# Perceiver block on one core: first chunks loaded one by one into four banks, and another order of TensorE's products in three steps of the self attention

## The chip, the core and the metric

The kernel runs on one core of a Trainium2 chip. The engines named below are TensorE (PE in the profile, PEld its weight loads), VectorE (DVE), ScalarE (ACT), GpSimd (POOL) and SyncE (SP, which here only issues DMAs). The metric is the device time of one execution in microseconds, lower is better.

## The reference

x is 8 sequences of 128 rows of 512, the context 8 x 2048 rows of 512. Three residual layers follow each other, each behind a layer norm:

```python
x = x + xattn(layernorm(x), ctx)   # q = x@Wq, k = ctx@Wk, v = ctx@Wv, 8 heads of 64, softmax, @Wo + bo
x = x + attn(layernorm(x))         # 8 heads in 2 groups, k and v through 32 latent columns, causal softmax, @wo
x = x + ffn(layernorm(x))          # gelu(x@W1)@W2 for all, and 2 of 8 experts for each row by its gate
```

All is float32. Where a product must be exact to about float32 and cheap, an operand is split in a rounded part (`_h`) and a rest (`_l`), and three products of the rounded type replace one.

## The kernel before

Every engine has its own written program, and semaphores join them; nothing reorders the work. The program has three parts: cross attention (to about 1045 us of the trace), self attention with the shared feed forward of the first six sequences (to about 1241 us), and the experts.

**Start of the cross attention.** The context comes in groups of 512 rows, a group in two parts of 512 KB (`load_ctx`, L217), each with two of the four 128-row chunks of the contraction; `stage[:, 0]` and `stage[:, 1]` hold the raw parts in turn. For the first group SP loads half of Wv, part 0, the other half, part 1 (L241 on). ScalarE rounds each as it lands (`first_part`, L605), VectorE makes the rest (L742, L745), counted by `wv_split` and `first_split`. TensorE's `project_v` (L401) makes a tile of 128 rows of values: 4 chunks x 3 products (`three`, L367), in one of two banks `ps_p` (`pair_ps` in the rows); `await_bank` lets it go on when the copy out of that bank, two tiles back, is done. `arrive_first` makes the first tile wait for each half. ScalarE copies tile 0, rounds parts 2 and 3 of the second group (`round_ctx`, L675), and then copies tiles 1 to 3 (`copy_v`, L626). GpSimd splits parts 2 and 3 (L300). Behind the first tile of the second group TensorE transposes x (`turn_x`, L483).

**Self attention.** Eight PSUM banks are handed around by a table: `fills(name, bank)` states in which order names fill a bank, `await_empty`, `await_filled` and `await_copied` wait by it. Before the loop over the eight sequences TensorE folds the weights (`fold_query_weights`, `turn_folded`, and `fold_out_weight` L1228, which makes `wol` from Wo), makes value latents of four sequences (`latents`, products with `wvd`), queries of four sequences (`queries`, products of `wql` and `xnT`, one half per bank and 8 products each in the rows' count), and scores of sequence 0. Half 1 stands for sequences 4 to 7. In step s of the loop: `turn_probs(s)` (transposes of `stage`), `scores(s+1)` (mask and L1272), `mix(s)` (L1291), `self_out(s)` (products with `wol`), `turn_norm` of the new row block (`x3T`, transposes of `xn`), `gate(s)` (products with `wg`), and `rank(s-1)` (L1308, L1309), which gives rows their places with the experts. Mixed in are the shared feed forward of earlier sequences: `up_high` and `up_low` of sequence s-1 (L1326, L1329, L1337), `turn_gelu`, `down_high` and `down_low` of sequence s-2 (L1354, L1361, L1364). Between self_out and x3T stand, on VectorE, the sum and its statistics, on GpSimd the root, and on VectorE the norm (L1570 to L1582); between `gate(s-1)` and `rank(s-1)` stand ScalarE's exponentials and VectorE's `choose` (L1711 on), which VectorE reaches only behind the norm of step s.

## Time and profile before

| | |
|---|---|
| median of 3 runs | 1548.08 us (1547.4 to 1550.31) |
| the profiled execution | 1547.3 us |
| its span | 1545.4 us |
| TensorE busy | 1503.8 us, 97% |
| VectorE, ScalarE, GpSimd busy | 723.2, 710.4 and 706.5 us |
| mean granted clock of TensorE | 0.994 |

The span runs from the first to the last instruction; the execution has 1.9 us around it. A matmul counts as busy from its issue to its modelled end, so neighbours overlap, and a row of the timeline that merges n of them lasts longer than the distance between their starts. Idle time in square brackets is that just before the row, with the instruction that ended it. An fp32 matmul of the program is two in the rows.

### The profile page before, as it was taken

The page shows a single profiled execution, that of the slowest core. Times are in us where ns is not written, and L with a number is a line of the kernel's source. Part 1 is how long each engine was busy: PE and PEld are TensorE (multiplying, and loading weights), DVE is VectorE, ACT ScalarE, POOL GpSimd, SP SyncE. Part 2 cuts the span into 40 slices and gives each one's busy share as a digit, 9 for nine tenths or more (in the row PEclk, how much of TensorE's full clock was granted, in tenths as well). Part 3 has the DMA queues.
Part 4 walks back from the last instruction along what each step waited for, and adds up shares of the span by engine and source line. Part 5 has one row for each costly group of instructions (what it writes and reads, how often), then busy time and mean ns, then how long its engine had stood idle before and what let it go on. Part 6 is the DMA issues. An engine that isn't in the chain of part 4 may idle for free. (4 is left out here: it accounts for less than half of the span.)

```text
span 1545.4 us, 25507 instructions
## 1 busy us (share of the span) xinstructions
PE 1503.8 (97%) x9986; PEld 1212.6 (78%) x9987; DVE 723.2 (47%) x1100; ACT 710.4 (46%) x1197; POOL 706.5 (46%) x559
## 2 busy tenths in 40 slices
PE   7999999999999999999999999989889999999997
PEld 5678888888888888888888888865567777888886
DVE  4124533632731822732543453393365565567552
ACT  3244544543644544454454454344466554454531
POOL 3112941851752572481392293076421116688651
PEclk9999999999999999999999999999899999999999
DMA  6111041022114103103104103115100076567522
GB/s 218 61 56 36 28 123 43 28 87 72 35 35 125 35 28 116 49 23 109 62 1 131 47 16 112 40 56 192 42 28 28 28 275 182 144 195 195 154 38 37
DMA packets 57446, 127.85 MB, mean 83 GB/s; under 512 B 7104, under 2 KB 11264, under 8 KB 57344
## 3 DMA queue, kind: packets, MB, share of 16 engines
q1 hardware_dynamic: 48672, 109.81, 22.0%
q0 software_dynamic: 4304, 8.44, 2.9%
q10 hardware_dynamic: 4368, 8.18, 1.8%
q8 instruction: 71, 1.16, 0.3%
q14 instruction: 31, 0.25, 0.1%
HBM read 94.22 MB, written 33.24 MB: 82 GB/s over the span
## 5 line engine op out<-in xcount | busy, mean ns | idle before, releaser
L300 POOL TENSOR_TENSOR ctx_l<-stage,ctx_h 128x1024 fp32r<-128x1024 f32 x62 | 147.5, 2401 | 481.9 <-ACT ctx_h L675 481.9
L367 PE MATMUL pair_ps<-wv,ctx_h 128*128 128x512 f32 x1024 | 323.4, 397 | 10.8 <-DVE ctx_l L745 9.3
L367 PE MATMUL pair_ps<-ctx_h,wk 128*128 128x512 f32 x1024 | 331.2, 394 | 0.0
L783 DVE TENSOR_TENSOR s_top<-ps_s,s_top 128x512 f32<-128x512 f32 x192 | 121.2, 684 | 338.8 <-ACT s L644 338.8
L367 PEld LDWEIGHTS pair_ps<-wv,ctx_h 128*128 128x128 f32 x1024 | 187.9, 188 | 54.0 <-issue 9.9
L367 PEld LDWEIGHTS pair_ps<-ctx_h,wk 128*128 128x128 f32 x1024 | 192.2, 188 | 42.7 <-issue 1.2
L626 ACT ACTIVATE vt<-pair_ps 128x512 f32<-128x512 f32 x128 | 76.5, 598 | 274.4 <-PE pair_ps L367 213.3
L367 PE MATMUL pair_ps<-wv,ctx_l 128*128 128x512 f32 x512 | 200.3, 391 | 0.0
L367 PE MATMUL pair_ps<-ctx_l,wk 128*128 128x512 f32 x512 | 199.5, 390 | 0.0
L644 ACT ACTIVATE s<-ps_s 128x512 f32<-128x512 f32 x256 | 133.0, 602 | 61.0 <-PE ps_s L420 36.6
L620 ACT ACTIVATE kT<-pair_ps 128x512 f32<-128x512 f32 x128 | 76.6, 598 | 176.7 <-PE pair_ps L367 176.7
L420 PEld LDWEIGHTS ps_s<-qT,kT 64*128 64x128 f32 x2048 | 119.3, 188 | 19.2 <-issue 16.5
L420 PE MATMUL ps_s<-qT,kT 64*128 64x128 f32 x2048 | 131.5, 278 | 0.0
L651 ACT ACTIVATE s<-s 128x1024 f32<-128x1024 f32 x128 | 125.8, 1049 | 4.6 <-DVE s L813 4.6
L785 DVE COPY s_top<-ps_s 128x512 f32<-128x512 f32 x64 | 40.4, 685 | 175.0 <-ACT s L644 175.0
L449 PEld LDWEIGHTS ps_o<-s,vt 128*64 128x64 f32 x2048 | 111.6, 137 | 5.0 <-issue 2.8
L449 PE MATMUL ps_o<-s,vt 128*64 128x128 f32 x2048 | 114.2, 273 | 1.2 <-ACT s L651 1.2
L367 PEld LDWEIGHTS pair_ps<-wv,ctx_l 128*128 128x128 f32 x512 | 96.5, 188 | 20.8
L367 PEld LDWEIGHTS pair_ps<-ctx_l,wk 128*128 128x128 f32 x512 | 96.2, 188 | 19.7 <-issue 1.2
L813 DVE TENSOR_TENSOR s<-s,ps_s 128x2048 f32<-128x2048 f32 x48 | 106.1, 2276 | 0.0
L2027 ACT ACTIVATE wxo<-pair_ps 128x512 f32<-128x512 f32 x46 | 27.6, 599 | 142.9 <-PE pair_ps L1967 142.3
L1876 POOL TENSOR_TENSOR lu<-raw_u,hu 128x1024 fp32r<-128x1024 f32 x28 | 69.2, 2815 | 28.5 <-ACT hd L2021 28.5
(295 smaller groups left out, 2323.2 us busy)
## 6 DMA issues: line engine op xcount, KB each, us to landing
stage<-in_ctx_dram SPq DMA_DIRECT2D x64, 512.0 KB, 4.1
rows_scratch<-bo SPq DMA_DIRECT2D x66, 258.5 KB, 4.7
raw_u<-in_up_dram SPq DMA_DIRECT2D x32, 512.0 KB, 3.9
stage<-in_down_dram SPq DMA_DIRECT2D x16, 512.0 KB
raw_e<-in_down_dram SPq DMA_DIRECT2D x16, 512.0 KB, 4.2
bo<-rows_scratch ACTq DMA_DIRECT2D x22, 258.5 KB, 3.2
s<-in_x_dram SPq DMA_DIRECT2D x2, 1024.0 KB, 11.5
q_scratch<-s SPq DMA_DIRECT2D x2, 1024.0 KB, 4.6
```

The lines of the kernel that those rows point to most:

```text
L300: nc.gpsimd.tensor_tensor(lo, raw, hi, ALU.subtract).then_inc(done, 1)
L367: mm = nc.tensor.matmul(out, w(c), m(c), start=(c + k == 0), stop=(c == DC - 1 and k == 2))
L420: mm = nc.tensor.matmul(ps_e[:, 2 * (n % 2) + e, i], kT[rows, p, i * P:(i + 1) * P], qT[rows, p, :], start=True, stop=True)
L449: mm = nc.tensor.matmul(ps_o[e * XD:(e + 1) * XD, p, :], vt[:, (b * MT + t) % RING, h * XD:(h + 1) * XD], s[:, h, t, :], start=(t == 0), s ...
L620: nc.scalar.activation(kT[:, p, :], ps_p[:, NTH[b, "K", g, p] % 2], ACT.Copy).then_inc(k_copied, 1)
L626: nc.scalar.activation(vt[:, nth_v(b, g, t) % RING, :], ps_p[:, NTH[b, "V", g, t] % 2], ACT.Copy) \
L644: nc.scalar.activation(s[:, 2 * p + e, 4 * g:4 * g + 4, :], ps_e[:, 2 * (n % 2) + e], ACT.Copy) \
L651: nc.scalar.activation(part, part, ACT.Exp, scale=X_SCALE).then_inc(exp_done, 1)
L783: ins = nc.vector.tensor_tensor(top[:, p, e], bank, top[:, p, e], ALU.max)
L785: ins = nc.vector.tensor_copy(top[:, p, e], bank)
L813: nc.vector.tensor_tensor(s[:, h], s[:, h], largest_score, ALU.subtract).then_inc(shifted, 1)
L1876: nc.gpsimd.tensor_tensor(weight_chunk(lu[s % 2], ld[s % 2], i), raw_part(i), weight_chunk(hu[s % 2], hd[s % 2], i), ALU.subtract).then_in ...
```

## The change

The first two chunks of Wv and of the context are loaded in four DMAs of 256 KB, each with a semaphore, and rounded and split singly; the other two chunks stay a pair. `first_values` takes chunk after chunk over all four tiles, which stand in four banks at once (`first_room`: two of `ps_p`, two of `ps_s`). So ScalarE copies all four at the end, behind the rounding of parts 2 and 3. Part 2 is loaded when the second chunk is split, part 3 when the last pair is.

In the self attention the folding of Wo moves behind the first scores, and its copies from ScalarE to VectorE. The first latents stand in two halves between other steps; the second latents move ahead of the loop, and half of the second queries into step 0 in their place. In step 1 `up_high(0, 0)` goes ahead of self_out and the rest of that sequence's up products ahead of `turn_norm`; from step 2 on the order is that of before. ScalarE rounds x3T of sequence 0 in step 0 (step 1 before), VectorE takes its rest ahead of the maxima of step 1. In the steps with a `down_high` that now stands ahead of `rank` where both are in front of self_out, which is so in the last step alone. The bank table follows.

```diff
@@ -238,12 +243,14 @@
 
-            for i in range(2):
-                load_weight(wv_raw, wv_ap, i, wv_in)
-                load_ctx(0, i)
+            for c, w_in, c_in in ((0, wv_start, ctx_start), (1, wv_in[0], raw_in[0])):
+                sp.dma_start(wv_raw[:, c, :], wv_ap[c * P:(c + 1) * P, :]).then_inc(w_in, 16)
+                sp.dma_start(stage[:, 0, c, :], ctx_ap[0, 0, :, c, :]).then_inc(c_in, 16)
+            load_weight(wv_raw, wv_ap, 1, wv_in)
+            load_ctx(0, 1)
             sp.dma_start(x_all[:, 0:HB], x_ap[0:HB].rearrange("b t d -> t b d")).then_inc(x_in[0], 16)
             for k in range(2, 4):
-                sp.wait_ge(first_split, k - 1)
+                sp.wait_ge(first_split, k)
@@ -369,17 +376,28 @@
 
-                if n >= 2:
+                if n in (4, 5):
+                    pe.wait_ge(v_copied, n - 3)
+                elif n >= 2:
                     b, kind, g, i = MADE[n - 2]
                     if kind == "K":
                         pe.wait_ge(k_copied, nth_k(b, g, i) + 1)
                     else:
                         pe.wait_ge(v_copied, nth_v(b, g, i) + 1)
 
-            def arrive_first(c):
-                if c % 2 == 0:
-                    pe.wait_ge(wv_split, c // 2 + 1)
-                    pe.wait_ge(first_split, c // 2 + 1)
+            def first_values():
+
+                for c in range(DC):
+                    if c < 3:
+                        pe.wait_ge(wv_split, c + 1)
+                        pe.wait_ge(first_split, c + 1)
+                    for t in range(4):
+                        rows = slice(t * P, (t + 1) * P)
+                        for k, (i, j) in enumerate(((ctx_h, 0), (ctx_l, 0), (ctx_h, 1))):
+                            mm = nc.tensor.matmul(first_room(t), i[:, 0, c, rows], wv[:, j, c, :], start=(c + k == 0),
+                                                  stop=(c == DC - 1 and k == 2))
+                        if c == DC - 1:
+                            mm.then_inc(proj_done, 1)
...
@@ -623,7 +640,8 @@
                     act.wait_ge(pv_done, PAIRS * (b if g or t == 3 else b - 1))
-                nc.scalar.activation(vt[:, nth_v(b, g, t) % RING, :], ps_p[:, NTH[b, "V", g, t] % 2], ACT.Copy) \
+                made = ps_p[:, NTH[b, "V", g, t] % 2] if b + g else first_room(t)
+                nc.scalar.activation(vt[:, nth_v(b, g, t) % RING, :], made, ACT.Copy) \
@@ -674,13 +692,13 @@
 
-            for i in range(2):
-                part = slice(2 * i, 2 * i + 2)
-                first_part(wv[:, 0, part, :], wv_raw[:, part, :], wv_in[i])
-                first_part(ctx_h[:, 0, part, :], stage[:, i], raw_in[i])
-            copy_v(0, 0, 0)
+            for c, w_in, c_in in ((0, wv_start, ctx_start), (1, wv_in[0], raw_in[0])):
+                first_part(wv[:, 0, c, :], wv_raw[:, c, :], w_in)
+                first_part(ctx_h[:, 0, c, :], stage[:, 0, c, :], c_in)
+            first_part(wv[:, 0, 2:4, :], wv_raw[:, 2:4, :], wv_in[1])
+            first_part(ctx_h[:, 0, 2:4, :], stage[:, 1], raw_in[1])
             round_ctx(0, (2, 3))
-            for t in range(1, 4):
+            for t in range(4):
@@ -736,13 +754,13 @@
 
-            for i in range(2):
-                part = slice(2 * i, 2 * i + 2)
+            for i, part in enumerate((slice(0, 1), slice(1, 2), slice(2, 4))):
+                raw = stage[:, 1] if i == 2 else stage[:, 0, part, :]
                 dve.wait_ge(first_hi, 2 * i + 1)
                 nc.vector.tensor_tensor(wv[:, 1, part, :], wv_raw[:, part, :], wv[:, 0, part, :], ALU.subtract) \
                     .then_inc(wv_split, 1)
                 dve.wait_ge(first_hi, 2 * i + 2)
-                nc.vector.tensor_tensor(ctx_l[:, 0, part, :], stage[:, i], ctx_h[:, 0, part, :], ALU.subtract) \
+                nc.vector.tensor_tensor(ctx_l[:, 0, part, :], raw, ctx_h[:, 0, part, :], ALU.subtract) \
...
@@ -1388,21 +1410,23 @@
             fold_query_weights(1)
-            pe.wait_ge(wo_in, 16)
             turn_folded(0)
-            fold_out_weight(0)
+            pe.wait_ge(wkv_in, 32)
+            latents(0, range(0, HB // 2))
             turn_folded(1)
-            fold_out_weight(1)
-            pe.wait_ge(wkv_in, 32)
-            latents(0)
+            latents(0, range(HB // 2, HB))
             for ro in range(2):
                 await_copied(pe, f"wql{ro}")
-            queries(0)
+            queries(0, range(SKV))
             pe.wait_ge(rounded, 2)
             scores(0)
+            pe.wait_ge(wo_in, 16)
+            for g in range(SKV):
+                fold_out_weight(g)
             for s in range(HB, B):
                 await_copied(pe, f"xT{s}")
-            queries(1)
+            queries(1, range(0, 1))
+            latents(1)
@@ -1415,26 +1439,32 @@
                 mix(s)
+                if 0 <= late < EARLY:
+                    down_high(late)
                 if s == B - 1:
                     rank(s - 1)
-                if 0 <= late < EARLY:
-                    down_high(late)
                 if s == 0:
                     keys(1)
+                if s == LAG:
+                    up_high(0, 0)
                 self_out(s)
                 if s == 0:
-                    latents(1)
+                    queries(1, range(1, SKV))
                 if 0 <= late < EARLY:
                     down_low(late)
-                if 0 <= soon < EARLY:
+                if 0 < soon < EARLY:
                     up_high(soon, 0)
+                if s == LAG:
+                    up_high(0, 1)
+                    up_low(0, 0)
+                    up_low(0, 1)
                 turn_norm(f"x3T{s}", s, B + s + 1)
-                if 0 <= soon < EARLY:
+                if 0 < soon < EARLY:
                     up_high(soon, 1)
                 if 0 < s < B - 1:
                     rank(s - 1)
                 gate(s)
-                if 0 <= soon < EARLY:
+                if 0 < soon < EARLY:
@@ -1506,14 +1536,12 @@
                 take(f"wql{n}", wql[:, :, n, :])
-                take(f"wol{n}", wol[:, n, :])
             take("vl0", vl[:, 0:HB])
             for ro in range(2):
                 take(f"ql0{ro}", qlT[:, ro, 0:HB * T])
             exps(0)
             normalise(0)
-            for ro in range(2):
-                take(f"ql1{ro}", qlT[:, ro, HB * T:B * T])
+            take("ql10", qlT[:, 0, HB * T:B * T])
@@ -1529,14 +1557,18 @@
                     take("vl1", vl[:, HB:B])
-                if 0 <= soon < EARLY:
-                    if soon:
-                        await_filled(act, f"up{soon - 1}{NH - 1}")
+                if 0 < soon < EARLY:
+                    await_filled(act, f"up{soon - 1}{NH - 1}")
                     await_copied(act, f"x3T{soon}")
                     nc.scalar.activation(rowT_h[:, :, :], x3T[:, soon % 2], ACT.Copy).then_inc(rowTh_done, 1)
                 if s + 1 < B:
                     normalise(s + 1)
+                if s == 0:
+                    take("ql11", qlT[:, 1, HB * T:B * T])
                 take(f"x3T{s}", x3T[:, s % 2])
+                if s == 0:
+                    await_copied(act, "x3T0")
+                    nc.scalar.activation(rowT_h[:, :, :], x3T[:, 0], ACT.Copy).then_inc(rowTh_done, 1)
@@ -1614,10 +1646,16 @@
             invert(0)
+            for g in range(SKV):
+                take(f"wol{g}", wol[:, g, :])
             dve.wait_ge(on_set, 3)
             for s in range(B):
                 late, soon = s - LAG - 1, s - LAG
                 take(f"pT{s}1", pT[:, 1])
+                if s == LAG:
+                    dve.wait_ge(rowTh_done, 1)
+                    nc.vector.tensor_tensor(rowT_l[:, :, :], x3T[:, 0], rowT_h[:, :, :], ALU.subtract) \
+                        .then_inc(rowTl_done, 1)
...
```

The order of the instructions is shown in three places. ScalarE, start of the cross attention, before:

```order
L605 ACTIVATE wv<-vt 128x1024 [waits wv_in0]
L605 ACTIVATE ctx_h<-stage 128x1024 [waits raw_in0]
L605 ACTIVATE wv<-vt 128x1024 [waits wv_in1]
L605 ACTIVATE ctx_h<-stage 128x1024 [waits raw_in1]
L626 ACTIVATE vt<-pair_ps 128x512 [waits proj_done]
L675 ACTIVATE ctx_h<-stage 128x1024 [waits raw_in0]
L675 ACTIVATE ctx_h<-stage 128x1024 [waits raw_in1]
L626 ACTIVATE vt<-pair_ps 128x512 [waits proj_done] x3
```

and now (rows of `vt` are the copies of value tiles, `wk` the rounding of Wk):

```order
L622 ACTIVATE wv<-vt 128x512 [waits wv_start]
L622 ACTIVATE ctx_h<-stage 128x512 [waits ctx_start]
L622 ACTIVATE wv<-vt 128x512 [waits wv_in0]
L622 ACTIVATE ctx_h<-stage 128x512 [waits raw_in0]
L622 ACTIVATE wv<-vt 128x1024 [waits wv_in1]
L622 ACTIVATE ctx_h<-stage 128x1024 [waits raw_in1]
L693 ACTIVATE ctx_h<-stage 128x1024 [waits raw_in0]
L693 ACTIVATE ctx_h<-stage 128x1024 [waits raw_in1]
L644 ACTIVATE vt<-pair_ps 128x512 [waits proj_done] x2
L644 ACTIVATE vt<-ps_s 128x512 [waits proj_done] x2
```

The first copy stood ahead of both later roundings of `ctx_h`; now all four stand behind them.

TensorE from the latents ahead of the loop to the end of step 0's self_out and what follows it, before (`xnT,wql` are queries, `wvd,xnT` latents, `wo,wupT` folding of Wo, `xnT,wkd` keys, `wol,o_mid` self_out):

```order
L1170 MATMUL pair_ps<-wvd,xnT 128x64 x16
L1170 MATMUL bank<-xnT,wql 128x512 x8
L1267 MATMUL bank<-mask_r,ident2r 128x512 x2
L1272 MATMUL bank<-wq,qlT 128x256 x4
L1170 MATMUL bank<-xnT,wql 128x512 x8
L1175 MATMUL bank<-ident,stage 128x128 x8
L1267 MATMUL bank<-mask_r,ident2r 128x512 x2
L1272 MATMUL bank<-wq,qlT 128x256 x4
L1291 MATMUL pair_ps<-o_mid,vl 32x128 x8
L1170 MATMUL bank<-xnT,wkd 128x512 x4
L1170 MATMUL pair_ps<-wol,o_mid 128x512 x2
L1170 MATMUL pair_ps<-wvd,xnT 128x64 x16
```

and now, from the second pair of products of the first scores on:

```order
L1294 MATMUL bank<-wq,qlT 128x256 x4
L1248 MATMUL pair_ps<-wo,wupT 32x512 x4
L1248 MATMUL bank<-wo,wupT 32x512 x4
L1190 MATMUL bank<-xnT,wql 128x512 x4
L1190 MATMUL pair_ps<-wvd,xnT 128x64 x16
L1195 MATMUL bank<-ident,stage 128x128 x8
L1289 MATMUL bank<-mask_r,ident2r 128x512 x2
L1294 MATMUL bank<-wq,qlT 128x256 x4
L1313 MATMUL pair_ps<-o_mid,vl 32x128 x8
L1190 MATMUL bank<-xnT,wkd 128x512 x4
L1190 MATMUL pair_ps<-wol,o_mid 128x512 x2
L1190 MATMUL bank<-xnT,wql 128x512 x4
```

The folding, half of the queries and the second latents now stand between the first scores and the transposes of the probabilities (`ident,stage`); behind self_out stand four products of queries where sixteen small ones of latents stood.

TensorE from the mix of step 1 to the transposes of step 2, before (`hu`, `lu` are the up products, `ident,xn` the transposes for x3T, `both,on` and `heap,on` rank, `wg,wqlT` gate):

```order
L1291 MATMUL pair_ps<-o_mid,vl 32x128 x8
L1170 MATMUL pair_ps<-wol,o_mid 128x512 x2
L1326 MATMUL bank<-hu,rowT_h 128x512 x4
L1329 MATMUL bank<-hu,rowT_l 128x512 x4
L1175 MATMUL bank<-ident,xn 128x128 x4
L1326 MATMUL bank<-hu,rowT_h 128x512 x4
L1329 MATMUL bank<-hu,rowT_l 128x512 x4
L1308 MATMUL pair_ps<-both,on 128x8
L1309 MATMUL pair_ps<-heap,on 128x8
L1170 MATMUL pair_ps<-wg,wqlT 128x8 x4
L1337 MATMUL bank<-lu,rowT_h 128x512 x8
```

and now:

```order
L1313 MATMUL pair_ps<-o_mid,vl 32x128 x8
L1348 MATMUL bank<-hu,rowT_h 128x512 x4
L1351 MATMUL bank<-hu,rowT_l 128x512 x4
L1190 MATMUL pair_ps<-wol,o_mid 128x512 x2
L1348 MATMUL bank<-hu,rowT_h 128x512 x4
L1351 MATMUL bank<-hu,rowT_l 128x512 x4
L1359 MATMUL bank<-lu,rowT_h 128x512 x8
L1195 MATMUL bank<-ident,xn 128x128 x4
L1330 MATMUL pair_ps<-both,on 128x8
L1331 MATMUL pair_ps<-heap,on 128x8
L1190 MATMUL pair_ps<-wg,wqlT 128x8 x4
```

All up products now stand ahead of the transposes of x3T; between these and rank, and between gate and the next step, nothing is left.

## Rows read from the trace of the kernel before

**Rows 1.** the timeline of the start: start us, us, engine, line, operation, count [idle before]
```profile
4.93 1.06 ACT L605 ACTIVATE wv<-vt 128x1024 fp32r<-128x1024 f32 x1 [2.90 <-DMA vt<-in_xv_dram]
...
6.89 1.06 ACT L605 ACTIVATE ctx_h<-stage 128x1024 fp32r<-128x1024 f32 x1 [0.90 <-DMA stage<-in_ctx_dram]
7.98 1.23 DVE L745 TENSOR_TENSOR ctx_l<-stage,ctx_h 128x1024 fp32r<-128x1024 f32 x1 [0.73 <-ACT ctx_h L605]
...
9.35 1.19 PE L367 MATMUL pair_ps<-wv,ctx_h 128*128 128x512 f32 x2 [9.35 <-DVE ctx_l L745]
...
10.63 1.23 DVE L745 TENSOR_TENSOR ctx_l<-stage,ctx_h 128x1024 fp32r<-128x1024 f32 x1
...
14.01 0.60 ACT L626 ACTIVATE vt<-pair_ps 128x512 f32<-128x512 f32 x1 [3.41 <-PE pair_ps L367]
```

**Rows 2.** the windows: line 367 alone from 14 to 19 us: length, PE busy, PEld busy, PEclk
```profile
14.00:19.00 5.00, 5.00 (x23) 4.13 (x23) 1.00 0.83 243
```

**Rows 3.** the timeline again, where the second context group begins
```profile
19.22 1.06 ACT L675 ACTIVATE ctx_h<-stage 128x1024 fp32r<-128x1024 f32 x1 [3.66 <-DMA stage<-in_ctx_dram]
20.19 1.07 ACT L626 ACTIVATE vt<-pair_ps 128x512 f32<-128x512 f32 x2
20.36 2.42 POOL L300 TENSOR_TENSOR ctx_l<-stage,ctx_h 128x1024 fp32r<-128x1024 f32 x1 [1.32 <-ACT ctx_h L675]
...
20.82 0.73 PE L367 MATMUL pair_ps<-wv,ctx_h 128*128 128x512 f32 x2 [1.40 <-ACT vt L626]
...
26.42 0.60 PE L483 MATMUL ps_m<-ident,s 128*128 128x128 f32 x4
```

**Rows 4.** TensorE's timeline, self attention, step 0 and ahead of it
```profile
1071.80 1.07 PE L1228 MATMUL bank<-wo,wupT 128*32 128x512 f32 x8
...
1087.27 7.13 PE L1170 MATMUL bank<-xnT,wql 128*128 128x512 f32 x16
1094.96 0.63 PE L1175 MATMUL bank<-ident,stage 128*128 128x128 f32 x4 [0.56 <-ACT stage L1479]
1096.13 0.63 PE L1175 MATMUL bank<-ident,stage 128*128 128x128 f32 x4 [0.54 <-ACT stage L1479]
...
1098.80 3.70 PE L1170 MATMUL bank<-xnT,wkd 128*128 128x512 f32 x8
...
1104.05 3.68 PE L1170 MATMUL pair_ps<-wvd,xnT 128*128 128x64 f32 x32
```

**Rows 5.** TensorE's timeline from the end of step 0 to step 2
```profile
1109.01 1.09 PE L1175 MATMUL bank<-ident,xn 128*128 128x128 f32 x4 [1.27 <-DVE xn L1582]
1111.11 1.85 PE L1170 MATMUL pair_ps<-wg,wqlT 128*128 128x8 f32 x8 [1.02 <-ACT wqlT L1452]
...
1119.82 1.95 PE L1170 MATMUL pair_ps<-wol,o_mid 128*128 128x512 f32 x4 [1.19 <-DVE o_mid L1564]
...
1127.41 0.63 PE L1175 MATMUL bank<-ident,xn 128*128 128x128 f32 x4 [3.16 <-DVE xn L1582]
...
1130.34 0.36 PE L1308 MATMUL pair_ps<-both,on 128*128 128x8 f32 x2 [0.47 <-DVE both L1716]
...
1133.61 1.03 PE L1175 MATMUL bank<-ident,stage 128*128 128x128 f32 x8
```

**Rows 6.** the timeline of VectorE and of ScalarE in step 0
```profile
1106.75 2.11 DVE L1582 TENSOR_SCALAR xn<-x_soon,mv,rstd 128x512 f32<-128x512 f32 x1 [0.67 <-POOL rstd L1157]
...
1108.05 2.44 ACT L1479 ACTIVATE stage<-stage,inv 128x128 f32<-128x128 f32 x8
```

**Rows 7.** the windows of all engines, for the granted clock (PEclk)
```profile
1108.00:1120.00 12.00, 8.79 (x47) 6.51 (x48) 3.98 (x10) 5.17 (x21) 2.98 (x2) 0.57 0.01 1
1245.00:1250.00 5.00, 5.00 (x20) 4.03 (x19) 1.27 (x8) 0.44 (x1) 0.31 (x1) 0.66 0.94 313
```

**Rows 8.** TensorE's timeline, last step of the self attention
```profile
1231.26 0.36 PE L1308 MATMUL bank<-both,on 128*128 128x8 f32 x2 [1.16 <-issue]
```

**Rows 9.** DMA issues: count, KB each, median us to landing
```profile
qT<-q_scratch SPq DMA_DIRECT2D x7, 256.0 KB, 2.9
```

33 lines of the change are left out of this document (20 added, 13 removed).

## The prediction

> **What bounds the kernel now.** I read the page first: TensorE is busy in nearly every slice, so the time is TensorE's work plus the places where it waits or runs at the lower clock. Then the waits of TensorE (who was waited for), which sent me to three stretches, and there the timeline, engine by engine; last the windows for the granted clock and the list of DMA issues. Four things are to be seen.
>
> At the start TensorE does nothing until 9.35: half of Wv and half of the first context group (512 KB each) are landed, rounded on ScalarE and split on VectorE in turn, 1.06 and 1.23 us apiece [rows 1]. Twelve products of the first tile then take from 9.35 to 14.01. Later 23 of them touch 5.0 us, so 22 starts, 0.227 apart [rows 2], so twelve would take 2.7: the cold start costs 1.9.
>
> Then, at 20.82, TensorE has waited 1.40 for a bank: ScalarE's copies of the value tiles stand behind the rounding of context part 3, whose transfer lands at 19.22 [rows 3].
>
> In steps 0 and 1 of the self attention TensorE waits seven times in rows of the timeline: 0.56 and 0.54 for the first probabilities, 1.27 for xn of step 0, 1.02 for the copy of its transpose (ScalarE is in the normalisation of step 1 until 1110.4), then 1.19, 3.16 and 0.47 in step 1 [rows 4, 5, 6]. From 1108 to 1120 the granted clock has a mean of 0.57, where it has 0.50 (1.2 GHz) or 1.00 (2.4 GHz) at a time: (1 - 0.57) / 0.5 x 12 = some 10.2 us at the lower level [rows 7].
>
> In the last step TensorE waits 1.16 for the choice of step 6 before `rank` [rows 8].
>
> **The change, part by part.** The profiled execution took 1547.3 us, span 1545.4 and 1.9 around it; the median before, 1548.1, is 0.8 above. All sums are made against 1547.3.
>
> *First chunks.* The first two DMAs become 256 KB each. A 256 KB load elsewhere lands in a median of 2.9 us [rows 9]; issued at 0.75 and 1.24 the second would be there at 4.1 at best, and at 4.9 at worst (ScalarE starts the first whole 512 KB part at 4.93). I take 4.9, because these loads start the queue. Half of 1.06 and half of 1.23, with 0.1 between, give 6.3 to 6.4 for the first product instead of 9.35: 3.0 earlier. The cold stretch is paid as before. Chunk 0 feeds 12 products (four banks), cold for 8 of them: to about 10.7; chunk 1 is split near 8.2 (1 MB are there at 6.89, then half of 1.06 and of 1.23), and chunks 2 and 3 at 11.86 as before [rows 1] (their transfers are not moved), when TensorE is still in chunk 1. So 48 products end at 6.4 + 1.9 + 48 x 0.227 = 19.2. No wait between.
>
> What is late next is part 3 again: it is requested after the last first split (third count now, second before), which is the same moment, so it lands at 19.2 as before. ScalarE now has both roundings ahead of all four copies, so: rounding to 20.3, first copy to 20.8, and TensorE can begin group 1 at 20.9; two of its four chunks take it to 22.3, and GpSimd's split of part 3 is done at 22.8 [rows 3]. The tile then ends at 22.8 + 1.4 = 24.2. Before, the x transposes behind the same tile began at 26.42. Gain 2.2. Behind the copies on ScalarE stands only the rounding of Wk, which waits for its own transfer. Everything after this in the cross attention is TensorE's own length, so the 2.2 should reach the end. Bounds: if part 3 still lands so late that TensorE needs it 1 us more, 1.2; if, with part 2 requested 1 us earlier, it lands before 17, then the end of the 48 products decides and the gain is 4.5.
>
> *Step 0.* The folding of Wo (two groups of 1.0 to 1.1) goes from before the queries to behind scores 0; so scores 0 end at 1085.3 instead of 1087.3 and the probabilities come 2.0 earlier. TensorE now has, behind them, folding 2.1, half of the second queries 3.3 (7.13 for both, tail included) and latents 3.6 [rows 4]: to 1094.2. The probabilities were there at 1094.9 and 1096.1, now 1092.9 and 1094.1: both waits vanish. From the first transposes to the end of self_out took 1094.96 to 1104.05, that is 8.55 without the 0.54: self_out ends at 1102.7 (1.35 earlier). Only 3.3 of queries stand behind it now, to 1106.0. xn came 4.96 after self_out's end (1104.05 to 1109.01), of which 2.11 is one VectorE operation [rows 6]; I leave it so: 1107.7, a wait of 1.6 in place of 1.27. ScalarE's normalisation began when the copy of the latents let it (1108.05); latents are early now, so it ends near 1106.3, the new copy of queries near 1106.9, and the x3T copy follows its transposes: `gate` starts at 1108.8, not 1111.11, and ends at 1109.7. The copies of the folded Wo move to VectorE (some 0.6 each, half of the 1.23 of its 128x1024 form [rows 1]), behind the inverses of step 0, 3 us ahead of `mix`: nothing.
>
> *Step 1.* At full clock transposes, scores and mix take 3.3 (1094.96 to 1098.80 without the 0.54), to 1113.0; the first half of up_high, eight products of 0.227, covers the 1.19 for u and its own wait; self_out, 1.7, ends at 1116.5. Ahead of the next transposes stand 16 such products, 3.6, against 4.96 for xn: a wait of 1.4 at 1120.1 where 3.16 stood. But nothing now stands between the transposes and `rank`: the choice on VectorE came 2.93 after them (1127.41 to 1130.34), so TensorE goes idle for 2.5 there, to 1124.4; rank and gate are 1130.34 to 1133.61 less the 1.8 of up_low, 1.5: to 1125.9. Before, the next transposes began at 1133.61 [rows 5]. At full clock that is 7.7 gained. Some 3.6 of it is the low clock of before (of its 10.2 us TensorE was busy for about 7, half of that lost), 4.1 are waits and drained pipelines.
>
> *The clock.* The clock fell before where TensorE had short waits and narrow products, and again between 1245 and 1250, there for (1 - 0.66) / 0.5 x 5 = 3.4 us of dense work [rows 7]. The new kernel still has such a stretch at 1106 to 1109.7 (idle 1.6 and 0.8, eight-column products) and has a new one at 1120.1 to 1125.9. So I charge two low stretches of 3.4, each with TensorE busy through it: 2 x 1.7 = 3.4. Bounds: none (0) and four of them (6.8). Term for both steps: 7.7 - 3.4 = 4.3, from 0.9 to 7.7.
>
> The Trainium skill (TensorE: Matmul & The Clock Gate, Part 1) ties the fall of the clock to an idle engine and its release to activity. Taken as idleness alone, the 3.16 us wait should have been the place of the fall; here the clock stayed at 1.00 there and fell after a 1.27 us wait, so the trace disagrees with that reading. By idleness alone the new kernel, with 2.5 as its longest wait there, would lose nothing to the clock: that is the second rival.
>
> *Last step.* down_high (1.9) goes ahead of `rank`, so the 1.16 is covered; VectorE's placing of rows follows rank and still ends before self_out does. Gain 1.1; bounds 0 and 1.2.
>
> Sum: 2.2 + 4.3 + 1.1 = 7.6. 1547.3 - 7.6 = 1539.7, and with the 0.8 to the median **1540.5 us**.
>
> **Rivals.**
> A. Absorbed start: the transfer of part 3, or its split, ends the start as before or later, and the first term is at most 1.0; the rest holds. For it: the transfer is what ScalarE waits for at 19.22. Against: the tile behind had 2.7 us of work that is now ahead of it. 1541.7 to 1542.7. Chance 0.15.
> B. No low clock in steps 0 and 1 (and part 3 perhaps earlier): 1548.1 - (2.2 + 7.7 + 1.1) = 1537.1, down to 1534.8. Chance 0.2.
> C. More low clock, four stretches of 3.4: 1543.9. For it: the new weak stretch is 5.8 us long, and before, one fall lasted three times as long as the other. Chance 0.15.
> D. Slower: the new idle 2.5 before `rank`, with rank and gate behind it, keeps TensorE at 1.2 GHz well into steps 2 to 4, whose work has no slack. It must eat 2.2 + 7.7 + 1.1 = 11.0, at half a us per us: above 22 us of low clock (10.2 before) the kernel is slower; at 30 us it is 1552.1. Against it: the one fall followed by dense products was over in 3.4. Chance 0.03.
> E. The clocks fall on other phases in the last step and behind it, which moves any case by 1.7 either way.
>
> **Numbers.** Forecast 0.47, A 0.15, B 0.2, C 0.15, D 0.03. The forecast's own range is 1538.8 to 1542.2; to hold 8 in 10 it reaches to most of A, B and C: 1536 to 1544.5. A measurement tells 0.2%, 3.1 us, from no change: faster than 1545.0 is all but D and a tail of C with E: faster 0.90, same 0.07, slower 0.03.
>
> **What would show it.** The first product at 6.4; no wait until about 19.2 and then one near 1.7 for a ScalarE copy; x transposes at 24.2. No wait for the first probabilities; waits of about 1.6, 0.8, 1.4 and 2.5 in steps 0 and 1; no wait before the last rank; the steps 2 to 6 as long as before. Wrong would be: a first product after 8, the transposes of x after 26, or low-clock stretches of more than 10 us in total between 1090 and 1140.

## The result, and the profile after

| | before | after |
|---|---|---|
| median | 1548.51 us (4 runs, 1547.4 to 1550.31) | 1539.74 us (4 runs, 1538.26 to 1541.63) |
| the profiled execution | 1547.3 us | 1541.63 us |
| its span | 1545.4 us | 1539.8 us |

The ratio is 0.9944, with a 95% interval of 0.9932 to 0.9955: the change takes 8.8 us off. The forecast was 1540.5. The profiled execution of before was the fastest of its kernel and that of after the slowest, so the two profiles lie only 5.7 us apart. What sets the profile of after apart is more time at the lower clock in steps 0 and 1, below; its other three executions have no profile.

**The start.** The timeline of the changed kernel (start us, length us, engine, line, operation, count, and in brackets the idle time before and who ended it) against [rows 1] and [rows 3]:

```profile
3.36 0.63 ACT L622 ACTIVATE wv<-vt 128x512 fp32r<-128x512 f32 x1 [1.33 <-DMA vt<-in_xv_dram]
...
5.14 0.63 ACT L622 ACTIVATE ctx_h<-stage 128x512 fp32r<-128x512 f32 x1 [1.15 <-DMA stage<-in_ctx_dram]
5.80 0.69 DVE L763 TENSOR_TENSOR ctx_l<-stage,ctx_h 128x512 fp32r<-128x512 f32 x1 [1.09 <-ACT ctx_h L622]
...
6.64 0.77 PE L397 MATMUL pair_ps<-wv,ctx_h 128*128 128x512 f32 x1 [6.64 <-DVE ctx_l L763]
...
8.15 0.63 ACT L622 ACTIVATE ctx_h<-stage 128x512 fp32r<-128x512 f32 x1 [0.98 <-DMA stage<-in_ctx_dram]
```

```profile
17.43 1.06 ACT L693 ACTIVATE ctx_h<-stage 128x1024 fp32r<-128x1024 f32 x1 [1.70 <-DMA stage<-in_ctx_dram]
18.40 1.06 ACT L644 ACTIVATE vt<-pair_ps 128x512 f32<-128x512 f32 x2
...
19.35 2.36 POOL L307 TENSOR_TENSOR ctx_l<-stage,ctx_h 128x1024 fp32r<-128x1024 f32 x1
```

```profile
18.95 0.40 PE L397 MATMUL ps_s<-wv,ctx_h 128*128 128x512 f32 x1
19.19 0.63 PE L374 MATMUL pair_ps<-wv,ctx_h 128*128 128x512 f32 x2
...
21.76 0.72 PE L374 MATMUL pair_ps<-wv,ctx_h 128*128 128x512 f32 x2 [1.03 <-POOL ctx_l L307]
...
23.25 0.60 PE L501 MATMUL ps_m<-ident,s 128*128 128x128 f32 x4
```

The first product starts at 6.64 (6.4 was said), and the 48 products run without a wait to 19.19 (19.2). There is no wait for a ScalarE copy behind them, because part 3 landed at 17.43 and not at 19.22. What ends the start now is GpSimd's split of part 3, at 21.7. The x transposes begin at 23.25, 3.2 us earlier than in [rows 3], where 24.2 was said. The eight kernels measured here whose start is that of after begin them at 23.25 to 24.01, 23.5 on average, and the three with the old start at 26.10 to 26.42, 26.3 on average: 2.7 us is the better figure for this term.

**Steps 0 and 1.** TensorE's timeline against [rows 4] and [rows 5]:

```profile
1083.69 3.70 PE L1190 MATMUL bank<-xnT,wql 128*128 128x512 f32 x8
1087.23 3.68 PE L1190 MATMUL pair_ps<-wvd,xnT 128*128 128x64 f32 x32
1090.75 1.04 PE L1195 MATMUL bank<-ident,stage 128*128 128x128 f32 x8
...
1104.03 0.63 PE L1195 MATMUL bank<-ident,xn 128*128 128x128 f32 x4 [1.35 <-DVE xn L1614]
1105.43 1.66 PE L1190 MATMUL pair_ps<-wg,wqlT 128*128 128x8 f32 x8 [0.78 <-ACT wqlT L1482]
...
1121.24 0.63 PE L1195 MATMUL bank<-ident,xn 128*128 128x128 f32 x4 [1.17 <-DVE xn L1614]
```

```profile
1101.71 1.89 POOL L1167 TENSOR_TENSOR hd<-wq,one 128x1024 fp32r<-128x1024 f32 x1
1101.78 2.11 DVE L1614 TENSOR_SCALAR xn<-x_soon,mv,rstd 128x512 f32<-128x512 f32 x1 [0.66 <-POOL rstd L1177]
...
1118.99 2.11 DVE L1614 TENSOR_SCALAR xn<-x_soon,mv,rstd 128x512 f32<-128x512 f32 x1 [0.67 <-POOL rstd L1177]
...
1121.48 1.89 DVE L1751 CAST xn<-index 128x2 f32<-128x2 uint32 x1
```

The probabilities' waits are gone (the transposes at 1090.75 have no bracket). The four waits that the prediction named can be read from who waited for whom between 1097 and 1130 us (us in total, times, the longest):

```profile
PE bank L1195 <- DVE xn L1614: 2.5, 2, 1.4
PE pair_ps L1330 <- DVE both L1754: 2.3, 1, 2.3
PE pair_ps L1190 <- ACT wqlT L1482: 0.8, 1, 0.8
```

(The first row holds two waits.) That is 1.35 for x3T0, 0.8 for gate, 1.17 for x3T1 (the timeline's bracket) and 2.3 for the rank, where 1.6, 0.8, 1.4 and 2.5 were said. The rows of VectorE and GpSimd above show what stands in two of these chains: xn at 2.11, as in [rows 6], beside an operation of GpSimd that starts just before it, and a cast of two columns at 1.89.

**The clock.** The windows, 1100 to 1135 us: length, then busy time of PE, PEld, DVE, ACT and POOL, the mean granted clock, DMA share and GB/s:

```profile
1100.00:1135.00 35.00, 29.42 (x150) 20.97 (x149) 19.60 (x51) 19.45 (x64) 12.07 (x9) 0.80 0.04 16
```

(1 - 0.80) / 0.5 x 35 = 14 us at 1.2 GHz. The same window of the kernel before has 0.85, 10.5 us. So in this execution there was more low clock than before, not the two stretches of 3.4 that the forecast charged. In windows of 1 us it is 6.8 us from 1105.6 on, behind the waits of step 0, and 6.8 from 1122.7 on, from within the wait for the rank. The prediction named more than 10 us of low clock between 1090 and 1140 as a sign that it was wrong; in this execution the sign was there.

**The last step.** TensorE waits 0.47 for gT_h ahead of down_high, which was not foreseen, and the wait of 1.16 before rank [rows 8] is gone:

```profile
1223.91 0.65 PE L1313 MATMUL pair_ps<-o_mid,vl 128*32 128x128 f32 x16
1225.04 2.09 PE L1376 MATMUL pair_ps<-hd,gT_h 128*128 128x512 f32 x8 [0.47 <-ACT gT_h L1553]
1226.96 0.28 PE L1330 MATMUL bank<-both,on 128*128 128x8 f32 x2
...
1232.76 0.60 PE L1195 MATMUL bank<-ident,xn 128*128 128x128 f32 x4
```

### The profile page after: what moved, and what is told of

Same layout as the page of the kernel before. It is cut to its first block and busy times, and to the rows that moved or that the text cites. A ratio compares the mean times of both kernels' runs of the same rounds, so it can differ in the third digit from the quotient of the medians.

```text
span 1539.8 us, 25515 instructions
## 1 busy us (share of the span) xinstructions
PE 1504.3 (98%) x9986; PEld 1214.8 (79%) x9987; DVE 722.1 (47%) x1104; ACT 709.9 (46%) x1197; POOL 705.5 (46%) x559
## 3 DMA queue, kind: packets, MB, share of 16 engines
q8 instruction: 71, 1.16, 0.3%
## 5 line engine op out<-in xcount | busy, mean ns | idle before, releaser
L374 PE MATMUL pair_ps<-wv,ctx_h 128*128 128x512 f32 x992 | 312.1, 396 | 1.0 <-POOL ctx_l L307 1.0
L374 PEld LDWEIGHTS pair_ps<-wv,ctx_h 128*128 128x128 f32 x992 | 181.3, 188 | 43.0 <-POOL ctx_l L307 1.5
L374 PE MATMUL pair_ps<-wv,ctx_l 128*128 128x512 f32 x496 | 193.6, 390 | 0.0
L637 ACT ACTIVATE kT<-pair_ps 128x512 f32<-128x512 f32 x128 | 76.6, 598 | 177.1 <-PE pair_ps L374 177.1
L438 PEld LDWEIGHTS ps_s<-qT,kT 64*128 64x128 f32 x2048 | 119.3, 188 | 19.2 <-issue 16.5
L374 PEld LDWEIGHTS pair_ps<-ctx_l,wk 128*128 128x128 f32 x512 | 96.2, 188 | 19.7 <-issue 1.2
L374 PEld LDWEIGHTS pair_ps<-wv,ctx_l 128*128 128x128 f32 x496 | 93.1, 188 | 20.0
```

The costliest lines, as they stand in the source:

```text
L374: mm = nc.tensor.matmul(out, w(c), m(c), start=(c + k == 0), stop=(c == DC - 1 and k == 2))
L438: mm = nc.tensor.matmul(ps_e[:, 2 * (n % 2) + e, i], kT[rows, p, i * P:(i + 1) * P], qT[rows, p, :], start=True, stop=True)
L637: nc.scalar.activation(kT[:, p, :], ps_p[:, NTH[b, "K", g, p] % 2], ACT.Copy).then_inc(k_copied, 1)
```

## The experiments

Twelve kernels were run; ratios are to the kernel before, from runs on the same chip. To compare the profiles I use one length: from the first folding of the query weights (products of `qlT` and `wupT`) to the first up_high of step 2, which holds all of steps 0 and 1. Both ends are starts of rows of TensorE's timeline; the waits are the brackets of the rows between them; low clock is the sum of (1 - PEclk) / 0.5 over windows of 1 us, all in us.

| kernel | median us | length | waits in it | low clock in it |
|---|---|---|---|---|
| before | 1548.5 | 81.6 | 9.3 | 10.2 |
| before, splits early | 1546.0 | 80.7 | 9.5 | 6.8 |
| start only | 1545.2 | 80.9 | 9.7 | 6.8 |
| self attention only | 1542.2 | 76.6 | 6.2 | 6.8 |
| **after** | 1539.7 | 79.2 | 6.3 | 13.6 |
| after, rank first | 1539.7 | 76.6 | 6.3 | 6.8 |
| after, part 3 on VectorE | 1538.0 | 76.6 | 6.3 | 6.8 |
| after, folding first | 1538.9 | 76.7 | 6.2 | 6.8 |
| after, step 1 old | 1539.0 | 76.1 | 7.4 | 3.4 |
| after, dense fill | 1535.0 | 73.5 | 2.2 | 0 |
| after, splits early | 1532.9 | 71.6 | 2.9 | 3.4 |
| after, splits between | 1530.6 | 68.7 | 1.9 | 0 |
| combined | 1528.8 | 68.6 | 1.8 | 0 |
| combined, step 1 old | 1532.7 | 71.4 | 4.5 | 0 |

Of the kernels with the order of after in steps 0 and 1 and nothing else changed there, three profiles show 6.8 us of low clock and a length of 76.6; only that of after itself has 13.6 and 79.2. The waits are the same in all four. "Part 3 on VectorE" has 3.4 us of low clock in each of the two steps, "self attention only" and "rank first" have none in step 0 and 6.8 in step 1, and after has 6.8 in both. What a wait does to the clock is thus not fixed by the wait.

The medians are over several executions, a length, its waits and its low clock are from one. Some profiles are at an end of their kernel's times: that of "after, step 1 old" is the fastest of five (1537.15 us at a mean clock of 0.997, the others 0.994), that of "after, splits early" the slowest of four (1533.81 at 0.994, the others 0.995 to 0.998). What an edit is worth is therefore taken from the medians, and the profiles tell where the time went.

### The two parts by themselves

The first applies only the part of the diff in the cross attention, the second only the part in the self attention.

> Only the start of the change (first chunks one by one, four banks); the self attention is that of the kernel before. Theory (the start is carried whole to the end): the x transposes begin at 23.2 instead of 26.42 and the cross attention behind them is TensorE's own length, so 3.1 to 3.2 us faster than the kernel before: 1545.3 against 1548.5. Rival (the gain is lost again at the next wait for DMA or for VectorE between the attentions, or the clock falls elsewhere for it): less than 1.5 us faster. If the whole change's 8.8 us is mostly start: over 5 us faster.

Measured: 1545.16 us (11 runs), ratio 0.9981 (0.9972 to 0.999), 3.25 us against the 1548.41 of before beside it. The theory's number; the rival's and the "mostly start" are out, the rival's just so, as the interval begins at 1.5 us. Not all of it need be the start: in its profile the x transposes begin at 23.74 and the first folding 2.4 us earlier than before, and steps 0 and 1 have 6.8 us of low clock where before has 10.2.

> Only the other order in the self attention (steps 0, 1 and the last); the start is that of the kernel before. Theory (terms add): whole change 8.8 less start 3.1 = 5.7 us faster than before, 1542.8, with waits of TensorE near 1.35, 0.8, 1.2 and 2.3 us in steps 0 and 1. By the profiled execution of the whole change alone (5.54 - 3.1 in steps 0 and 1, 0.7 in the last) it would be 3.1 us faster: 1545.4. The difference between the two is the number of low-clock stretches: with four of 3.4 us in steps 0 and 1 the low figure, with two the high one. Rival (the two parts need each other): under 2 us faster.

Measured: 1542.18 us, ratio 0.9962 (0.9948 to 0.9975), 6.2 us. The waits are those of after, the low clock is 6.8 us, and the length is 5.0 shorter than before. The parts sum to 9.5 where the whole gives 8.8; the intervals are over 1 us wide each way, so they add as far as this can tell.

### The last step undone

```
                 mix(s)
-                if 0 <= late < EARLY:
-                    down_high(late)
                 if s == B - 1:
                     rank(s - 1)
+                if 0 <= late < EARLY:
+                    down_high(late)
```

> The changed kernel with one edit taken back: in the last step TensorE does rank again ahead of down_high (as in the kernel before). Theory (down_high covers the wait for the choice): a wait of about 1.1 us before rank comes back and the 0.47 for gT_h goes, 0.7 slower than the changed kernel: about 1540.4 against 1539.7, and in the profile the x3T transposes of the last step 0.7 later from the step's start. Rival (the choice is late by less than down_high anyway, or VectorE decides the end of the step): no difference, and then nothing is seen in the profile either.

Measured: 1539.68 us, ratio 0.995 (0.9936 to 0.9963): no difference that the times can show. The timeline of this kernel does:

```profile
1221.50 0.65 PE L1313 MATMUL pair_ps<-o_mid,vl 128*32 128x128 f32 x16
1223.31 0.36 PE L1330 MATMUL bank<-both,on 128*128 128x8 f32 x2 [1.16 <-issue]
...
1231.07 0.60 PE L1195 MATMUL bank<-ident,xn 128*128 128x128 f32 x4
```

From mix to the x3T transposes it takes 9.57 us. After has 1223.91 and 1232.76 for them, 8.85 (above). The edit is worth 0.7, not the 1.1 predicted: down_high itself waits 0.47 for gT_h, which rank had covered.

### Step 0: where the folding stands

```
+            pe.wait_ge(wo_in, 16)
+            for g in range(SKV):
+                fold_out_weight(g)
...
             queries(0, range(SKV))
...
             scores(0)
-            pe.wait_ge(wo_in, 16)
-            for g in range(SKV):
-                fold_out_weight(g)
```

> The changed kernel with one edit of step 0 undone: the two foldings of Wo stand ahead of the first queries again, not behind the first scores. The scores then end 2.0 us later, and the first probabilities with them, while TensorE's work up to their transposes is the same. In the changed kernel ScalarE was done with them at 1088.6 and TensorE came at 1090.75. Theory (2.2 us of slack, of which 2.0 are used): no wait, or one under 0.3; no difference, 1539.4 to 1540.1. Rival (the foldings behind the scores are what covers the first probabilities, as the prediction has it): waits of 0.56 and 0.54 as before and 1 us or more slower, 1540.7 or more.

Measured: 1538.91 us, ratio 0.9943 (0.9929 to 0.9957). No wait came back: in its timeline the transposes of the probabilities start at 1091.10, straight behind the latents. But this does not show that the move is worth nothing. The work between the scores and these transposes is now 7.05 us (1084.05 to 1091.10), as long as the 7.1 of before (1087.27 to 1094.40), where both waits stood. What differs is VectorE, which makes the negated maxima in between. Before, and in this kernel:

```profile
1088.09 2.17 DVE L1591 TENSOR_SCALAR nmx<-mx 128x4 f32<-128x4 f32 x1
...
1090.89 1.23 DVE L1591 TENSOR_SCALAR nmx<-mx 128x4 f32<-128x4 f32 x1
```

```profile
1084.88 0.17 DVE L1623 TENSOR_SCALAR nmx<-mx 128x4 f32<-128x4 f32 x1
...
1085.67 1.72 DVE L1623 TENSOR_SCALAR nmx<-mx 128x4 f32<-128x4 f32 x1
...
1091.10 1.04 PE L1195 MATMUL bank<-ident,stage 128*128 128x128 f32 x8
```

The two take 3.40 us before and 1.89 here, 1.5 less, and from the first maximum to the start of the normalisation it is 6.2 us before and 4.7 here: this alone is enough for the waits to go, and it comes from how these two operations meet GpSimd's splits. In after itself the pair takes 1.40, and 8.9 us of TensorE's work stand behind the scores (1081.84 to 1090.75). Before, the second four transposes stood 8.9 us behind the scores' end; in after they come 9.3 behind it (the first four take 0.4). So the longer work of the new order would cover the probabilities even with the maxima of before (an estimate from these rows), and no run separates the two causes.

### Step 1: the old order

> The changed kernel with step 1 of the self attention back in the order of before (up_high of step 0's rows behind self_out and behind the transposes, up_low behind gate); start, step 0 and last step as changed. Theory by its waits: one of about 1.2 for u before self_out comes back and the wait for x3T1 grows from 1.17 to about 3.0, while that before rank goes from 2.28 to about 0.4: 1.1 us more waiting, 1540.8 against 1539.7. The clock decides the rest: the new order's second low-clock stretches lie in step 1, behind its thin transposes, rank and gate; if the old order keeps them away, up to 3 us come back: 1537.5 to 1540. Rival (step 1's order carries most of the change's gain in the self attention, 6 us): 1543 or more.

Measured: 1539.01 us, ratio 0.9941 (0.9928 to 0.9955). Within a microsecond of after, on the lower side. The waits in the new place are as expected (row by row: 1.62 for u, 2.95 for x3T1), 1.1 us more than in after, but only 3.4 us of low clock, in a profile that is this kernel's fastest execution. By the medians the new order of step 1 was worth nothing in the changed kernel that can be told from the noise, and the gain in the self attention is step 0's. Against before, 1.9 us of the shorter length are waits and 3.4 (half of 6.8) low clock.

### Dense work in the waits

```
...
-                    queries(1, range(1, SKV))
+                    queries(1, range(1, SKV), 2)
...
-                    up_high(0, 1)
+                    up_high(0, 1, 4)
+                turn_norm(f"x3T{s}", s, B + s + 1)
+                if s == LAG:
                     up_low(0, 0)
                     up_low(0, 1)
-                turn_norm(f"x3T{s}", s, B + s + 1)
```

The third argument of queries repeats its first products (1.35 us of them), that of up_high does its rowT_h products four times (12 more, 0.227 each).

> The changed kernel with products done twice over (their bank is started again, so the result stands) where TensorE waits in steps 0 and 1: 1.35 us of them ahead of x3T0, 0.9 ahead of x3T1, and both up_low (1.8 us) moved behind the x3T1 transposes into the wait for the rank, with 1.8 us of repeats in their old place. Nothing waits for these products that didn't wait before. Theory (it is the thin work around these waits that lets the clock fall): low-clock time in steps 0 and 1 falls from 13.65 us to at most one or two stretches of 3.4, 2 to 4 us faster, 1535.5 to 1538. Rival (the waits are what costs, and the clock falls with other things): the same low-clock time, and no change or up to 1 us slower, since the fill overruns the waits by little: 1539.5 to 1541.

Measured: 1534.99 us, ratio 0.9913 (0.9898 to 0.9928), 4.7 us less than after by doing 4 us more of useless work. The window 1100 to 1135 of this kernel:

```profile
1100.00:1135.00 35.00, 33.47 (x187) 23.34 (x186) 23.56 (x62) 23.05 (x74) 12.68 (x10) 1.00 0.05 16
```

The clock stays at 2.4 GHz throughout. Nothing was taken out of any other engine's chain, so the gain is the clock's. That the few us of idle time in these two steps let the clock fall is thereby shown. The thin products beside them (transposes, eight-column gates, rank) are still there and with the waits filled did not lower the clock; whether they are needed for it to fall was not tested, and what exactly the chip counts is not shown. The Trainium skill (TensorE: Matmul & The Clock Gate, Part 1, "A second HAM failure mode") tells of a kernel in which many small idle times between groups of products made the clock go down and up; this kernel agrees with that passage, and not with long idleness as the only cause.

### GpSimd's last two splits

```
-            for i in range(CH - 2):
+            for i in range(CH):
                 split(i)
...
-                if s < 2:
-                    split(CH - 2 + s)
```

> The changed kernel, but GpSimd does its last two weight splits (4.3 us each) in the 9.8 us in which it is idle ahead of step 0, and not behind the roots of steps 0 and 1. Theory (the waits of steps 0 and 1 are VectorE's chain, stretched by GpSimd's splits on the memory port they share): the xn operations take 0.55 instead of 2.11 us and the cast of the choice 0.2 instead of 1.89; the wait for x3T0 (1.35) goes, that for x3T1 (1.17) goes, and that before the first rank shrinks from 2.28 to about 0.6 (2.28 - 1.7); together 3.5 to 4.2 us, and 1 to 3 more if low-clock stretches go with the waits: 1533 to 1536 against 1539.7. Rival (xn and the cast take their time whatever GpSimd does, or the splits then hold something up at the softmax of step 0): no change or slower, 1539 to 1541.

Measured: 1532.87 us, ratio 0.9898 (0.9882 to 0.9913), 6.9 us less than after. The timeline of VectorE in this kernel:

```profile
1093.29 0.69 DVE L1619 TENSOR_REDUCE mx<-bank 128x4 f32<-128x512 f32 x1 [0.76 <-PE bank L1292]
1094.02 1.66 DVE L1621 TENSOR_SCALAR nmx<-mx 128x4 f32<-128x4 f32 x1
1095.59 0.68 DVE L1619 TENSOR_REDUCE mx<-bank 128x4 f32<-128x512 f32 x1
...
1102.48 0.55 DVE L1612 TENSOR_SCALAR xn<-x_soon,mv,rstd 128x512 f32<-128x512 f32 x1 [0.67 <-POOL rstd L1177]
...
1111.00 0.17 DVE L1621 TENSOR_SCALAR nmx<-mx 128x4 f32<-128x4 f32 x1
...
1118.05 0.17 DVE L1749 CAST xn<-index 128x2 f32<-128x2 uint32 x1
```

and of GpSimd:

```profile
1093.29 2.36 POOL L1170 TENSOR_TENSOR ld<-wq,hd 128x1024 fp32r<-128x1024 f32 x1
```

xn went from 2.11 to 0.55, the cast from 1.89 to 0.17. The splits now meet the negated maxima, 1.66 where 0.17 is their length alone, while the tensor_reduce that starts with the same split keeps its 0.69. Of the waits named, those for x3T0 and x3T1 went and that for the rank is 0.32, but 0.53 came for o_mid before self_out, and that before gate grew from 0.78 to 1.34. The Trainium skill (SBUF — State Buffer, "Who interferes with whom") says that copies, casts and tensor_scalar in their two-port modes wait for GpSimd's whole instruction at a shared pair of ports, and that tensor_reduce never does; these rows agree with both.

The next kernel places the two splits between VectorE's small operations:

```
...
             for i in range(CH - 2):
                 split(i)
+            split(CH - 2, (nmx_done, 2 * SKV))   # its second half waits for the maxima of step 1
...
-                if s < 2:
-                    split(CH - 2 + s)
+                if s == 0:
+                    pool.wait_ge(xn_done, B + 1)
+                    split(CH - 1)
```

> The changed kernel with GpSimd's last two splits in other places: the first in its idle time ahead of step 0, its second half held back until VectorE has written the negated maxima of step 1, the last behind the xn of step 0. Against the kernel with both splits early, in which these small VectorE operations took 1.66 and 1.23 us beside a split (0.17 alone) and ScalarE's softmax of step 1 ran late, so that TensorE waited 1.34 before gate. Theory (the shared port alone stretched them): 0.17 us each, the wait before gate falls to 0.3 or less, no wait for x3T1 or rank over 0.5; 0.5 to 1.5 us faster than the 1532.9 of that kernel: 1531.4 to 1532.4. Rival (something else makes ScalarE late, or the last split now lies on operations of step 1): 1533 or more.

Measured: 1530.56 us, ratio 0.989 (0.9875 to 0.9905), 2.3 less than with both splits early; more than the 0.5 to 1.5 expected. The length is 2.9 shorter: 1.0 of waits, and most of the rest the low clock that went too. In its timeline x3T0 has no wait, but gate waits 0.83 and not 0.3 or less: ScalarE's copy of the transposes (0.59 of it) stands there whatever VectorE does.

```profile
1102.74 0.60 PE L1199 MATMUL bank<-ident,xn 128*128 128x128 f32 x4
1104.17 1.03 PE L1194 MATMUL pair_ps<-wg,wqlT 128*128 128x8 f32 x8 [0.83 <-ACT wqlT L1486]
```

The early splits were also put into the kernel before.

> The kernel before, whole, with only GpSimd's last two splits moved into its idle time ahead of step 0. It tells what the new order of TensorE is worth once VectorE is no longer held up. Theory (order and splits attack the same waits in part: before, xn cost waits of 1.27 and 3.16 us, of which 1.56 each is the port): 3 to 5 us faster than the kernel before, 1543.4 to 1545.4; the changed order then keeps 7 or more of its own against it (1532.9, and 3.2 of that is the start). Rival (the order only covered what the port had stretched): over 9 us faster, 1539.5 or less, and the new order would be worth nothing beside it.

Measured: 1545.97 us (11 runs), ratio 0.9985 (0.9976 to 0.9994): 2.1 less than the 1548.02 of before beside it, less than the 3 to 5 of my theory. The timelines of VectorE and TensorE say why:

```profile
1098.69 1.66 DVE L1589 TENSOR_SCALAR nmx<-mx 128x4 f32<-128x4 f32 x1
...
1100.97 1.84 DVE L1589 TENSOR_SCALAR nmx<-mx 128x4 f32<-128x4 f32 x1
...
1103.29 1.96 PE L1168 MATMUL pair_ps<-wol,o_mid 128*128 128x512 f32 x4 [1.15 <-DVE o_mid L1562]
1105.08 3.68 PE L1168 MATMUL pair_ps<-wvd,xnT 128*128 128x64 f32 x32
1108.60 0.61 PE L1173 MATMUL bank<-ident,xn 128*128 128x128 f32 x4
1112.13 1.84 PE L1168 MATMUL pair_ps<-wg,wqlT 128*128 128x8 f32 x8 [2.93 <-ACT wqlT L1450]
```

The wait for xn went (1.27 in [rows 5]), and the one for ScalarE right behind it grew from 1.02 to 2.93: in the old order ScalarE gets the latents of the second half only after self_out, and its normalisation follows them. A wait of 1.15 for o_mid is new too: the early splits now meet the negated maxima of step 1, 1.66 and 1.84 us, where before they took 0.17 each. All waits together are no less than before (9.5 against 9.3), and the gain is low clock. So moving the splits early gives 2.1 there and 6.9 in the new order. Part of that difference is this placing, which costs 1.15 of wait in the old order and 0.53 in the new; the old order with the splits between was not run, so how much the two edits help each other is open.

### Part 3 on VectorE, and all of it together

```
             root(0)
-            split_ctx(0, 3)                          # GpSimd
...
             statistics(0)                            # VectorE
+            dve.wait_ge(hi_done, 2)
+            dve.wait_ge(split_done, 3)
+            nc.vector.tensor_tensor(ctx_l[:, 1, 2:4, :], stage[:, 1],
+                                    ctx_h[:, 1, 2:4, :], ALU.subtract).then_inc(split_done, 1)
             normalise(0)
```

> The changed kernel, but the low part of context part 3 is made by VectorE (1.23 us for a 128x1024 subtraction) right behind its first statistics, not by GpSimd (2.36 us, behind its root). Theory (after the change the start ends on GpSimd's split of part 3, not on the 48 products and not on the bank): the wait of 1.03 us at 20.6 goes and the x transposes start at 22.2 instead of 23.25, so 1.0 us faster: 1538.7. Rival (the transfer of part 3 or VectorE's normalisation of x, now later, holds the start at the same place): x transposes at 23.0 or later, 1539.5 to 1540.

Measured: 1538.0 us, ratio 0.9938 (0.9924 to 0.9951), 1.7 less than after, of which the profile shows 1.07. The timeline of this kernel:

```profile
18.82 1.23 DVE L852 TENSOR_TENSOR ctx_l<-stage,ctx_h 128x1024 fp32r<-128x1024 f32 x1 [0.25 <-ACT ctx_h L692]
...
19.96 1.92 DVE L781 TENSOR_SCALAR s<-s,mv,rstd 128x512 f32<-128x512 f32 x4
...
22.18 0.60 PE L500 MATMUL ps_m<-ident,s 128*128 128x128 f32 x4
```

The transposes are 1.07 earlier, as expected. The four normalising operations take 1.92 here; beside GpSimd's split in after they took 3.97.

> The changed kernel with what gained so far together: splits placed between VectorE's small operations (1530.6 alone), part 3's low half on VectorE (1538.0 alone, against 1539.7), and ScalarE taking x3T0 ahead of the copy of the last queries. Theory (the first two terms lie at opposite ends of the kernel and add; the third is hidden behind the transposes, as ScalarE is free only 0.1 us earlier than they are done): 1530.6 - 1.1 to 1.7 = 1529.2, from 1528.9 to 1529.6. Rival (the phases of the clock, or a later wait in the cross attention, eat the start's gain): 1530.5 or more.

Measured: 1528.83 us (1528.7 to 1529.29), ratio 0.9875 (0.986 to 0.989). This kernel beats both: 19.7 us less than before and 10.9 less than after. The third edit in it, ScalarE's order in step 0, was not run alone; it leaves the wait before gate at 0.78 (0.83 without it), and the 1.7 against the kernel with the splits between is what part 3 gave by itself.

> The combined kernel (1528.8) with step 1 of the self attention in the order of before. In the changed kernel itself that edit was worth nothing (1539.0 with the old order, 1539.7 with the new). Theory (there the new order's gain was taken back because VectorE's stretched xn and cast left thin work between two waits, and the clock fell): with VectorE free, the old order's waits of 1.6 for u and about 1.4 for x3T1 come back against 0.4 before rank, and perhaps a low-clock stretch with them: 2.0 to 4.5 us slower than the combined kernel, 1530.8 to 1533.3. Rival (step 1's order is worth nothing in any case): 1528.8 within 1 us.

Measured: 1532.73 us, ratio 0.9901 (0.9886 to 0.9916), 3.9 slower than the combined kernel. The length is 2.7 longer, all of it waits (4.5 against 1.8: 1.62 for u, 1.39 for x3T1) and none of it low clock; the other microsecond is not in steps 0 and 1 (its window from 1220 to 1245 has a clock of 0.86, that of the combined kernel 0.93). So the new order of step 1 is worth 2.7 to 3.9 us when VectorE is not held up, and nothing that shows when it is.

## Why the prediction was right

**First chunks (2.2 said; 3.2 in the profile of after, 2.7 on average).** The mechanism was right up to 19.2. Its premise that the last first split stays at 11.86 was not: that split ends at 13.13, 0.6 us before TensorE comes to chunk 2, so it cost nothing. The failing step is "so it lands at 19.2 as before". SyncE's two requests for parts 2 and 3 end at 13.48 (below; 12.22 in the kernel before), so part 3 was asked for 1.3 us later, and landed 1.8 us earlier. With ScalarE free, its copies were out of the way when TensorE came, and the named wait of 1.7 never was; GpSimd's split ended the start, at 21.7 and not 22.8. Why the transfer was faster was not tested, so the better result of this term is luck. The range given (1.2 to 4.5) holds it. Rival A is out by the run with the start alone. SyncE's timeline of after:

```profile
9.53 3.95 SPq L222 DMA_DIRECT2D stage<-in_ctx_dram  x2
```

**Steps 0 and 1 (4.3 said; 5.0 in the profile with the self attention alone).** The four waits were said as 1.6, 0.8, 1.4, 2.5 and came as 1.35, 0.78, 1.17, 2.28. The 2 x 3.4 us of low clock charged are the sum that three of four profiles with this order show, but only one of the three has them in both steps; in the others all 6.8 lie in step 1. That 4.3 and 5.0 lie so close is in part luck: the profile of before had 10.2 us of low clock, and that of "start only", with the same order there, 6.8 and a length of 80.9. The forecast also counted seven waits in these steps; a small one of 0.38 for rowT_h (at 1122.16 in the kernel before) was passed over, and nothing in the sum rests on it. The reason given for the probabilities, more work behind earlier scores, fits the rows; it did not see that the maxima of before were stretched, which is enough to make the waits. The run with the old order of step 1 corrects more. The forecast took from step 1 a large part of its 7.7 us; by the medians that step gave nothing in the changed kernel. Its waits were only moved: 1.62 and 2.95 with the old order, 1.17 and 2.28 with the new.

**The clock.** The forecast's sum goes by half a microsecond for each one at 1.2 GHz in which TensorE works. The table allows a test of this: the kernels without low clock have a length less waits of 66.8 (68.6 - 1.8) and 66.9 (71.4 - 4.5). Self attention only: 76.6 - 6.2 - 66.8 = 3.6 for 6.8 us, where 3.4 was said. After: 79.2 - 6.3 - 66.8 = 6.1 for 13.6, of which 1.4 lie in the wait for the rank, so 6.1 would be due. For the new order the price holds. With the old order of step 0 something is left over: before has 5.5 for 10.2, the start alone and the kernel before with early splits 4.4 and 4.4 for 6.8, about 1 us more than the price in each of the last two. Some of that is the drained pipeline: the last product before a wait counts 0.39 where the next would start 0.227 behind it, and these kernels have 9 or 10 waits where those above have 4 to 6 (an estimate: 0.16 each, 0.5 to 1 us). Rivals B and C differ from the forecast only in how much low clock there is, and this differs between profiles with the same order and the same waits: the profile of after was C's case, with 13.6 us. The sum charged two stretches by where it saw weak ones; the profiles show that this fixes neither their place nor their length, so that the median came near the forecast and not near C is in part luck.

**Last step (1.1 said, 0.7 measured).** A wait of 0.47 for gT_h was overlooked. This is the second step that failed: "the 1.16 is covered" is so, but down_high has a wait of its own.

**Rival D** (low clock on into steps 2 to 4) did not come. The steps 2 to 6 take as long as before, 82.04 us in both from the first up_high of step 2 to the probabilities' transposes of step 7; the windows of after from 1135 to 1170 and to 1220 have a clock of 1.00 and TensorE busy throughout.

**The sum.** 7.6 was said and 8.8 came in the medians. With 2.7 for the start and 0.7 for the last step, 5.4 are left for steps 0 and 1, within the 0.9 to 7.7 given; the profiles have 2.4 to 5.0 against the 81.6 of before, according to how much low clock they hold. So two terms were too small (by 0.5 and 1.1) and one too large (0.4). The forecast of 1540.5 is only 0.8 above the median because it started from 1548.1 where the median of before is now 1548.5.
